# One stage of a fused transformer kernel: the ReLU's bias add goes to GpSimd, and the two copies of each expert block out of PSUM go from ScalarE to VectorE

## The chip, the cores and the metric

The kernel runs on one core of one Trainium2 chip. The metric is the device time of one execution in microseconds (us); before the change it is 1316.74 us, the median of three runs (1316.6 to 1319.15). A core has five engines that run side by side, each through its own list of instructions in order: TensorE (PE in the rows, with PEld for its weight loads), VectorE (DVE), ScalarE (ACT), GpSimd (POOL) and SyncE (SP, which only issues DMAs here). They wait for each other by semaphores. Matmul results land in PSUM; GpSimd does not touch PSUM in this kernel.

## What is computed

The reference is a two-layer network on 4 x 512 tokens of 128 features. The part that matters here is layer 0: a differential attention over 8 heads, and beside it a mixture of 8 experts, of which each token uses one:

```python
L1 = einsum(l2norm(q1), l2norm(k1)) * cos_scale;  L2 = einsum(l2norm(q2), l2norm(k2)) * cos_scale
G  = tanh(delta_gain * (L1 - L2))
A1 = softmax(L1 + G);  A2 = softmax(L2 - G)
y  = einsum(A1 - lambda_full * A2, v)             # then RMS norm, projection
...
idx = argmax(xf @ Wg.T)                           # one expert per token
h = relu(xf @ W1[e] + b1[e]);  out += (idx == e) * (h @ W2[e] + b2[e])
```

After it come a second part of layer 0 and layer 1 (a four-layer Mamba stack and a top-2 mixture of experts), which the change does not touch.

## The kernel before

The kernel is written as stages, each a `Block` in which every engine's list is written out by hand; nothing schedules the instructions but the order of the code and the semaphores. The change lies in the second stage (from about 104 to 342 us), which runs the attention of the 8 heads and, woven into it, the experts.

**Attention.** A pair of heads takes 32 steps, four steps to a unit (one batch, four key tiles), so 8 units to a pair; four pairs run one after the other. Each step needs, on TensorE, one matmul for L1 - L2 (`difference`, bank_d) and two for L1 and L2 (`scores`, bank_l); on ScalarE one tanh (`gate`, L932) and, for two steps together, one exp (`exps_of_two`, L939); on VectorE the two sums L1 + G and -L2 - G (`sums`, L988 and L989), which read bank_l. Once a unit the exps are multiplied with the values (`weigh`, L863), ScalarE copies the result out of bank_pv (`keep`, L944), TensorE transposes it (`turn`, L871) and VectorE folds it into `ybig` (`settle`, L996). `weigh` of the next unit may only write bank_pv after `settle`.

**Experts.** Tokens are sorted by expert into 24 blocks of 128 rows, one per unit of the last three pairs (the first pair instead computes the sort, writes the rows out by indirect DMA and fetches the first weights). A block goes through one PSUM bank, bank_e: TensorE transposes it (`turn_block`, L838), ScalarE copies it out (`keep_in`, L948), TensorE multiplies with W1 (`hidden`, L844), VectorE adds the bias and takes the ReLU in four instructions, one per 128 columns (`relu`, L1004), TensorE multiplies with W2 (`block_out`, L850), ScalarE copies the result out (`keep_out`, L953), SyncE stores it. GpSimd fetches the weights of the block after the next (L752, L755), once `block_out` has finished with the buffer.

**Other small work.** After each head VectorE scales its values and squares them for the RMS norm in six instructions spread over six steps (`norm_head`, L1053 to L1065). GpSimd sets up the gain and the values of the head after the next (`next_head`, L746 and L749), after the last `weigh` of the old one. SyncE loads the queries and keys of later heads, twelve DMAs per head, into XT (first head of a pair) or GATE (second).

On TensorE the order in a unit is: turn_block, weigh (first half), two differences, hidden, scores, weigh (second half), scores, two differences, block_out, scores, turn, scores. TensorE takes them strictly in that order, so a step that is not ready holds up all behind it.

Of the kernel before, what the change touches and what calls it, by code (L numbers as in the profile page):

```python
# [7 lines left out]
ALU = mybir.AluOpType  # L8
# [3 lines left out]
P = 128  # L12
# [35 lines left out]
def build_stages(nc, A, out):  # L48
    keep = ExitStack()
    with keep:  # L50
# [24 lines left out]
        with keep0:  # L75
# [556 lines left out]
            with st2:  # L632
# [44 lines left out]
                s_hn = sem("head_norm_steps")  # L677
# [9 lines left out]
                loaded = lambda q, k: q * (8 * PER) + 16 * (k // 2 + 1)  # L687

                with nc.Block() as block:
                    @block.sync  # L690
                    def _(sp):
# [48 lines left out]
                        for i in range(2):  # L740
                            sp.wait_ge(s_es[i], 16 + loaded(2, PER - 2))

                    @block.gpsimd
                    def _(pool):
# [6 lines left out]
                        def gather_weights(q, j, i, n):  # L751
# [4 lines left out]
                                                         bounds_check=NE * P - 1, oob_is_err=False).then_inc(s_wl[i], 16)  # L756

# [16 lines left out]
                        pool.sem_inc(s_cur, LEAD)  # L774
# [9 lines left out]
                        next_head(-1, 0)  # L784
                        next_head(-1, 1)

                        def turn(q, more):
# [132 lines left out]
                    def _(act):  # L920
                        for s in (s_G, s_E, s_pvs, s_xk, s_ek):
                            act.sem_inc(s, LEAD)
                        for s in s_es:
                            act.sem_inc(s, 16)
# [21 lines left out]
                        def keep_in(q, k):  # L946
                            act.wait_ge(s_xt, blk(q, k + 1))
                            nc.scalar.activation(xbT[:, :], bank_e[:, 0, :], ACT.Copy).then_inc(s_xk, 1)  # L948

                        def keep_out(q, k):  # L950
                            act.wait_ge(s_dn, blk(q, k + 1))
                            act.wait_ge(s_es[k % 2], loaded(q, k))
                            nc.scalar.activation(eo[k % 2][:, :], bank_e[:, 0, :], ACT.Copy).then_inc(s_ek, 1)  # L953

                        def pair_of_heads(q, first=False, final=False):
                            for st in range(0, STEPS, 2):
# [4 lines left out]
                                if mb == 0 and not first:  # L961
                                    keep_in(q, u)
# [3 lines left out]
                                if mb == 2 and not first:  # L966
                                    keep_out(q, u)
# [10 lines left out]
                    def _(dve):  # L978
                        for s in (s_T, s_yb, s_relu):
                            dve.sem_inc(s, LEAD)  # L980
                        link = Chain(dve, s_dch)
# [18 lines left out]
                        def relu(q, k):  # L1000
# [47 lines left out]
                        def norm_head(h, n, settled, done):  # L1048
                            seg = ybig[:, :, bass.ds(h * 34, 34)].rearrange("p t (s c) -> p t s c", s=2)
                            plus, minus = seg[:, :, 0, 0:16], seg[:, :, 1, 0:16]  # L1050
                            if n == 0:
                                dve.wait_ge(s_yb, settled)
                                nc.vector.reciprocal(rz[:, :, :].unsqueeze(3), seg[:, :, :, 16:17]).then_inc(s_hn, 1)  # L1053
                                return
                            dve.wait_ge(s_hn, done + n)
                            if n == 1:
                                nc.vector.tensor_scalar(rz[:, :, 1], rz[:, :, 1], neg_lam[:, :], None, ALU.mult).then_inc(s_hn, 1)
                            if n == 2:
                                TT(seg[:, :, :, 0:16], seg[:, :, :, 0:16], rz[:, :, :].unsqueeze(3).broadcast_to([P, NT, 2, 16]), ALU.mult).then_inc(s_hn, 1)
                            if n == 3:  # L1060
                                TT(plus, plus, minus, ALU.add).then_inc(s_hn, 1)
                            if n == 4:
                                TT(ysq[:, :, :], plus, plus, ALU.mult).then_inc(s_hn, 1)
                            if n == 5:
                                nc.vector.tensor_reduce(ms[:, :, bass.ds(h, 1)], ysq[:, :, :].unsqueeze(2), AX.X, ALU.add).then_inc(s_hn, 1)  # L1065
# [1520 lines left out]
```

## Time and profile before

| | us |
|---|---|
| median of three runs (lowest, highest) | 1316.74 (1316.6, 1319.15) |
| the profiled execution's own time | 1318.12 |
| its span, first to last instruction | 1316.3 |
| the 24 expert units, first turn_block to the last | 164.28 to 332.29 |

A row of the timeline gives the start, the duration, the engine, the source line, the operation, and in brackets how long the engine had been idle before it and what ended that wait. SPq rows are DMA issues. A row with "x8" is eight instructions merged, and its duration runs from the first one's start to the last one's end.

Over the whole span the page has TensorE busy for 87%, VectorE for 84%, ScalarE for 79% and GpSimd for 69%, at a mean granted clock of 0.953. Most of GpSimd's work lies in later stages; in this one it is idle for most of the time.

### The profile page before, as it was taken

To read this page: it belongs to the slowest core of one execution; us is meant where nothing else is said; L and a number is where in the kernel's file an instruction comes from. 1 tells how busy PE (TensorE), PEld (TensorE's weight loads), DVE (VectorE), ACT (ScalarE), POOL (GpSimd) and SP (SyncE) were. 2 spreads that over 40 slices of the span, in tenths; PEclk is the share of its full clock that TensorE was granted. 3 is DMA by queue.
4 is the path that set the end of the run, shared out by engine and by line. 5 is a ranking of instruction groups with operands and counts; after the bars stand their busy time and mean duration, and the time that the engine had idled before them with its cause. 6 is when DMAs were issued, how large, how long until landed. Compare 5 with 4: busy or idle time off the path is not lost. (4 is left out here: it accounts for less than half of the span.)

```text
span 1316.3 us, 21647 instructions
## 1 busy us (share of the span) xinstructions
PE 1145.7 (87%) x6667; PEld 611.3 (46%) x6667; DVE 1101.3 (84%) x1535; ACT 1043.2 (79%) x1804; POOL 912.4 (69%) x749
## 2 busy tenths in 40 slices
PE   6566799999719999977999999999999999999885
PEld 4461244444515656753444444444444444444442
DVE  8967899999675323339999999999999999999997
ACT  4346999999452224378999999999999999999992
POOL 6733311111473451367999999999999999999995
PEclk9786999999858999998999999999999999999998
DMA  2022233433108216434144414442442354234420
GB/s 71 33 88 95 77 107 113 126 114 104 31 23 287 88 36 163 129 85 101 54 107 106 99 45 104 104 98 56 104 112 68 74 107 113 59 77 105 107 65 16
DMA packets 89060, 120.19 MB, mean 91 GB/s; under 512 B 17869, under 2 KB 49464, under 8 KB 88576
## 3 DMA queue, kind: packets, MB, share of 16 engines
q1 hardware_dynamic: 82688, 101.59, 30.4%
q0 software_dynamic: 6272, 17.38, 4.5%
q8 instruction: 48, 0.79, 0.3%
q14 instruction: 52, 0.43, 0.1%
HBM read 92.28 MB, written 27.45 MB: 91 GB/s over the span
## 5 line engine op out<-in xcount | busy, mean ns | idle before, releaser
L2104 POOL TENSOR_TENSOR hcm<-hs,Cc 128x1024 f32<-128x1024 f32 x255 | 600.3, 2376 | 27.8 <-DVE hs L2487 19.8
L2487 DVE TENSOR_TENSOR_SCAN hs<-decay,dbx 128x512 f32<-128x512 f32 x512 | 586.9, 1201 | 25.6 <-ACT decay L2380 9.9
L2221 PEld LDWEIGHTS dbx<-ident_sb,scaled 128*128 128x128 f32 x2048 | 227.4, 142 | 288.7 <-DVE hs L2487 164.8
L2221 PE MATMUL dbx<-ident_sb,scaled 128*128 128x128 f32 x2048 | 312.1, 283 | 41.6 <-DVE hs L2487 38.2
L2362 ACT ACTIVATE scaled<-duT,BT 128x256 f32<-128x256 f32 x579 | 266.9, 506 | 0.2 <-PE dbx L2221 0.2
L2380 ACT ACTIVATE decay<-dtr_even,a_all 128x512 f32<-128x512 f32 x256 | 179.0, 723 | 3.0 <-DVE hs L2487 1.7
L2380 ACT ACTIVATE decay<-dtr_odd,a_all 128x512 f32<-128x512 f32 x256 | 177.7, 719 | 2.4 <-DMA dtr_odd<-dt_turn 1.5
L2239 PE MATMUL y_bank<-hcm,fold_sb 128*32 128x512 f32 x1024 | 138.9, 615 | 1.8 <-POOL hcm L2104 1.8
L939 ACT ACTIVATE ex<-tt 128x2048 f32<-128x2048 f32 x64 | 123.8, 1934 | 2.5 <-DVE tt L989 1.8
L2152 PE MATMUL slots<-XT,w_tap 128*128 128x512 f32 (+1 forms) x224 | 115.5, 597 | 3.1 <-DVE scaled L2478 2.9
L988 DVE TENSOR_TENSOR tt<-bank_l,gt 128x512 f32<-128x512 f32 x128 | 87.1, 681 | 12.7 <-ACT gt L932 10.9
L2089 POOL TENSOR_SCALAR scaled<-duT,BT 128x256 f32<-128x256 f32 x204 | 95.3, 479 | 0.0
L932 ACT ACTIVATE gt<-bank_d,dgh 128x512 f32<-128x512 f32 x128 | 82.7, 714 | 10.2 <-PE bank_d L817 9.2
L989 DVE SCALAR_TENSOR_TENSOR tt<-bank_l,gt 128x512 f32<-128x512 f32 x128 | 87.1, 680 | 0.0
L1849 DVE TENSOR_TENSOR hid<-sil,u_bank 128x512 f32<-128x512 f32 x32 | 22.0, 687 | 59.1 <-ACT sil L1706 37.5
L863 PE MATMUL bank_pv<-ex,v_head 128*32 128x512 f32 x512 | 69.1, 612 | 2.0 <-DVE ybig L996 1.7
L752 POOL CAST weight_rows<-w_row 128x1 uint32 (+1 forms) x24 | 4.7, 195 | 95.1 <-PE bank_e L850 95.1
L2478 DVE TENSOR_TENSOR scaled<-slots,BT 128x1024 f32<-128x1024 f32 (+1 forms) x60 | 67.9, 1131 | 0.0
L1706 ACT ACTIVATE sil<-g_bank 128x512 f32<-128x512 f32 x32 | 19.1, 597 | 47.3 <-PE u_bank L1563 47.2
L1939 DVE TENSOR_TENSOR hid<-sil,u_bank 128x320 f32<-128x320 f32 x32 | 15.6, 488 | 48.8 <-ACT sil L1792 48.8
L1527 POOL DMA_INDIRECT shares_of_tokens<-eo,to_u x18 | 17.2, 954 | 51.9 <-ACT eo L1829 48.3
L1519 POOL DMA_INDIRECT expert_rows<-XR,rows_u x32 | 31.3, 978 | 30.9 <-PE o_bank L1570 21.6
(379 smaller groups left out, 1882.3 us busy)
## 6 DMA issues: line engine op xcount, KB each, us to landing
Cc<-bc_turn SPq DMA_DIRECT2D x256, 64.0 KB, 2.2
dtr_even<-dt_turn SPq DMA_DIRECT2D x32, 512.0 KB, 8.7
dtr_odd<-dt_turn SPq DMA_DIRECT2D x32, 512.0 KB, 8.3
dt_turn<-dt SPq DMA_DIRECT2D x16, 512.0 KB, 2.8
hid<-in_conv_row SPq DMA_DIRECT2D x4, 512.0 KB, 5.4
shares_of_tokens<-zeros SPq DMA_DIRECT2D x2, 1024.0 KB, 7.9
w_rg<-in_w_rg SPq DMA_DIRECT2D x8, 256.0 KB, 3.0
w_ru<-in_w_ru SPq DMA_DIRECT2D x8, 256.0 KB, 3.8
```

What stands on the lines that cost most here:

```text
L932: nc.scalar.activation(gt[:, st % RING, :], bank_d[st % 2][:, :], ACT.Tanh, scale=dgh[:, i:i + 1]).then_inc(s_G, 1)
L939: nc.scalar.activation(ex[:, (st // 4) % 2, j:j + 2, :, :], tt[:, i:i + 2, :, :], ACT.Exp).then_inc(s_E, 2)
L988: nc.vector.tensor_tensor(tt[:, st % RING, 0, :], bank_l[st % 2][:, 0, :], gt[:, st % RING, :], ALU.add)
L989: nc.vector.scalar_tensor_tensor(tt[:, st % RING, 1, :], bank_l[st % 2][:, 1, :], -1.0, gt[:, st % RING, :], ALU.mult, ALU.subtract).then_ ...
L2089: nc.gpsimd.tensor_scalar(scaled[buffer_of(l, n, k)][:, kk, :, j, :], duT[:, n % 2, kk, :].rearrange("p (g c) -> p g c", c=32), BT[:, n % ...
L2104: nc.gpsimd.tensor_tensor(hcm[:, r - 1:r + 1, :], hs[:, p % HR - 1:p % HR + 1, :], Cc[:, k:k + 1, :].broadcast_to([P, 2, 512]), ALU.mult). ...
L2152: last = mm(dst[h][:, d:512], w_tap[:, 3 - d, P * h:P * h + P], XT[:, n % 4, 0:512 - d], start=(d == 0), stop=(d == 3))
L2221: last = nc.tensor.transpose(dbx[bank_of[p]][:, P * kk:P * kk + P], scaled[buffer_of(l, b, k)][:, kk, g, :, :].rearrange("p j c -> p (j c) ...
L2239: last = mm(y_bank[h][32 * q:32 * q + 32, :], fold[:, :], hcm[:, ring_of(l, b, p + q), :], start=False, stop=(k == 3), tile_position=(0, 3 ...
L2362: nc.scalar.activation(scaled[buffer_of(l, n, k)][:, kk, :, j, :], duT[:, n % 2, kk, :].rearrange("p (g c) -> p g c", c=32), ACT.Copy, sca ...
L2380: nc.scalar.activation(dec[:, p % DR, :], dtr[b % 2][:, g, :], ACT.Exp, scale=a_all[:, l, 4 * g + k:4 * g + k + 1]).then_inc(s_dec, 1)
L2487: nc.vector.tensor_tensor_scan(hs[:, p % HR, :], dec[:, p % DR, :], dbx[bank_of[p]][:, :], 0.0, ALU.mult, ALU.add).then_inc(s_sc, 1)
```

## The change

The change does five things, all in the second stage:

1. The bias. relu(z + b) is written as max(z, -b) + b. VectorE does the first half for all 512 columns in one instruction (`floor_at_bias`), GpSimd adds b afterwards in SBUF (`add_bias`), and only then may `block_out` start. GpSimd waits for a new semaphore, `s_floor`.
2. `keep_in` and `keep_out` move from ScalarE to VectorE. `keep_out` of the block before stands after the sums of a unit's second step and ahead of `settle`; `keep_in` stands after `settle`, ahead of the sums of the third step.
3. Four of the six instructions of `norm_head` move to GpSimd (`weigh_head`); VectorE keeps the reciprocal (steps 5 and 21) and the closing reduction (now at steps 14 and 30).
4. SyncE issues the loads of head 2 (`first_head_of_next(-1, .)`) ahead of its wait for the sorted rows, no longer behind it.
5. Semaphore counts follow. The first `keep_out` copies a bank that holds nothing yet and stores nothing; the last one stands after the pairs.

```diff
                         for part in range(2):
                             load_part(sp, 1, 1, part, s_ld[1])
+                        for part in range(2):
+                            first_head_of_next(-1, part)
                         sp.wait_ge(s_scat, 16 * NT)
                         for i in range(AHEAD):
                             load_block(i, i)
-                        for part in range(2):
-                            first_head_of_next(-1, part)
...
+                        def weigh_head(h, done):
+                            seg = head_values(h)
+                            plus, minus = seg[:, :, 0, 0:16], seg[:, :, 1, 0:16]
+                            pool.wait_ge(s_hn, done)
+                            pool.sem_inc(s_asked, 1)
+                            nc.gpsimd.tensor_scalar(rz[:, :, 1], rz[:, :, 1], neg_lam[:, :], None, ALU.mult).then_inc(s_hn, 1)
...
                         next_head(-1, 0)
+                        weigh_head(0, 1)
                         next_head(-1, 1)
+
+                        def add_bias(q, k):
+                            pool.wait_ge(s_floor, blk(q, k + 1))
+                            pool.sem_inc(s_asked, 1)
+                            nc.gpsimd.tensor_tensor(hid[:, :, :], hid[:, :, :], b1[k % 2].unsqueeze(2).broadcast_to([P, 4, P]), ALU.add).then_inc(s_relu, 1)
 
                         def turn(q, more):
                             for k in range(PER):
+                                add_bias(q, k)
+                                if k == 2:
+                                    weigh_head(q * 2 + 1, q * 12 + 7)
                                 if k == PER // 2 and more:
                                     next_head(q, 0)
+                                if k == 6:
+                                    weigh_head(q * 2 + 2, q * 12 + 13)
...
-                                if mb == 0 and not first:
-                                    keep_in(q, u)
...
-                                if mb == 2 and not first:
-                                    keep_out(q, u)
...
+                        def keep_out(q, k):
+                            dve.wait_ge(s_dn, blk(q, k + 1))
+                            dve.wait_ge(s_es[k % 2], loaded(q, k + 2))
+                            nc.vector.tensor_copy(eo[k % 2][:, :], bank_e[:, 0, :]).then_inc(s_ek, 1)
+
+                        def floor_at_bias(q, k):
                             dve.wait_ge(s_h, blk(q, k + 1))
                             dve.wait_ge(s_wl[k % 2], loaded(q, k))
-                            for f in range(4):
-                                last = nc.vector.tensor_scalar(hid[:, f, :], bank_e[:, f, :], b1[k % 2][:, f:f + 1], 0.0, ALU.add, ALU.max)
-                            last.then_inc(s_relu, 1)
+                            nc.vector.scalar_tensor_tensor(hid[:, :, :], b1[k % 2].unsqueeze(2).broadcast_to([P, 4, P]), -1.0, bank_e[:, :, :],
+                                                           ALU.mult, ALU.max).then_inc(s_floor, 1)
...
+                                if mb == 2 and not first:
+                                    keep_in(q, u)
                                 sums(q, st)
+                                if mb == 1 and not first:
+                                    keep_out(q, u - 1)
                                 if mb == 1 and not (first and u < 2):
                                     settle(q, u - 2)
...
+                                if st == 14 and not first:
+                                    mean_square(q * 2 + 1, q * 12 + 11)
```

TensorE's order is the same before and after. On VectorE a unit without norm work (the first of the last pair; bank_l0 and bank_l1 are the two banks of scores, block_out1 the buffer of the block before) stands like this before:

```order
L988 TENSOR_TENSOR tt<-bank_l1,gt 128x512
L989 SCALAR_TENSOR_TENSOR tt<-bank_l1,gt 128x512
L996 TENSOR_REDUCE ybig<-bank_pv 128x4x34
L988 TENSOR_TENSOR tt<-bank_l0,gt 128x512
L989 SCALAR_TENSOR_TENSOR tt<-bank_l0,gt 128x512
L988 TENSOR_TENSOR tt<-bank_l1,gt 128x512
L989 SCALAR_TENSOR_TENSOR tt<-bank_l1,gt 128x512
L1004 TENSOR_SCALAR hid<-bank_e,expert_weights0 128x128 x4
```

and like this after:

```order
L1006 TENSOR_TENSOR tt<-bank_l1,gt 128x512
L1007 SCALAR_TENSOR_TENSOR tt<-bank_l1,gt 128x512
L1025 COPY block_out1<-bank_e 128x128
L1014 TENSOR_REDUCE ybig<-bank_pv 128x4x34
L1020 COPY block_inT<-bank_e 128x128
L1006 TENSOR_TENSOR tt<-bank_l0,gt 128x512
L1007 SCALAR_TENSOR_TENSOR tt<-bank_l0,gt 128x512
L1006 TENSOR_TENSOR tt<-bank_l1,gt 128x512
L1007 SCALAR_TENSOR_TENSOR tt<-bank_l1,gt 128x512
L1030 SCALAR_TENSOR_TENSOR hid<-expert_weights0,bank_e 128x512
```

So one copy stands ahead of `settle`, the other between `settle` and the four sums, and one instruction of 512 columns takes the place of four of 128.

On GpSimd the first three blocks of the last pair are, before (a cast and a gather per block):

```order
L752 CAST weight_rows0<-w_row 128x1
L755 DMA expert_weights0<-in_w_expert,weight_rows0 128x1028
L752 CAST weight_rows1<-w_row 128x1
L755 DMA expert_weights1<-in_w_expert,weight_rows1 128x1028
L752 CAST weight_rows0<-w_row 128x1
L755 DMA expert_weights0<-in_w_expert,weight_rows0 128x1028
```

and after:

```order
L810 TENSOR_TENSOR hid<-hid,expert_weights0 128x512
L754 CAST weight_rows0<-w_row 128x1
L757 DMA expert_weights0<-in_w_expert,weight_rows0 128x1028
L810 TENSOR_TENSOR hid<-hid,expert_weights1 128x512
L754 CAST weight_rows1<-w_row 128x1
L757 DMA expert_weights1<-in_w_expert,weight_rows1 128x1028
L810 TENSOR_TENSOR hid<-hid,expert_weights0 128x512
L765 TENSOR_SCALAR rz2<-rz2,neg_lam 128x16
L768 TENSOR_TENSOR ybig<-ybig,rz2 128x16x2x16
L771 TENSOR_TENSOR ybig<-ybig 128x16x16
L774 TENSOR_TENSOR ysq2<-ybig 128x256
```

Each block begins with the bias add, and the norm work of a head stands behind that of the third (and seventh) block. At the turn from one pair to the next, the add of the new pair's first block stands behind `next_head`, which waits for the old pair's last `weigh`.

On SyncE, between the loads of head 1 (into GATE) and the loop, the loads of head 2 (into XT) follow the two block loads before:

```order
L109 DMA GATE<-qk_parts 8x2048
L701 DMA block_in0<-block_rows 128x128
L701 DMA block_in1<-block_rows 128x128
L107 DMA XT<-qk_parts 24x1x2048
L107 DMA XT<-qk_parts 16x1x2048
```

and precede them after:

```order
L109 DMA XT<-qk_parts 24x1x2048
L109 DMA XT<-qk_parts 16x1x2048
L109 DMA XT<-qk_parts 8x2048
L703 DMA block_in0<-block_rows 128x128
L703 DMA block_in1<-block_rows 128x128
```

The twelve loads of head 2 thus no longer stand behind the wait for the sorted rows.

## Rows read from the trace of the kernel before

**Rows 1.** Busy time by engine: 24 expert units, then one unit (window, length first)

```profile
core 0: us, PE busy (x) PEld busy (x) DVE busy (x) ACT busy (x) POOL busy (x), PEclk, DMA share, GB/s
164.28:332.29 168.01, 162.93 (x1128) 82.16 (x1128) 157.16 (x336) 158.19 (x209) 29.13 (x54) 1.00 0.37 111
310.46:317.47 7.01, 7.01 (x51) 3.58 (x50) 6.39 (x14) 6.84 (x10) 1.20 (x3) 1.00 0.32 96
```

**Rows 2.** Timeline, TensorE and VectorE in that unit (start, us, engine, line)

```profile
309.55 0.66 PE L871 MATMUL bank_pv<-ident_sb,pvs 128*128 128x128 f32 x4
...
310.25 0.44 DVE L996 TENSOR_REDUCE ybig<-bank_pv 128x136 f32<-128x272 f32 x1 [0.46 <-PE bank_pv L871]
...
310.46 0.33 PE L838 MATMUL bank_e<-ident_sb,block_in 128*128 128x128 f32 x1
...
310.84 0.69 DVE L988 TENSOR_TENSOR tt<-bank_l,gt 128x512 f32<-128x512 f32 x1 [0.16 <-ACT gt L932]
...
312.18 1.06 PE L844 MATMUL bank_e<-block_inT,expert_weights 128*128 128x128 f32 x8
...
313.28 1.13 DVE L1004 TENSOR_SCALAR hid<-bank_e,expert_weights 128x128 f32<-128x128 f32 x4
...
315.25 1.06 PE L850 MATMUL bank_e<-expert_weights,hid 128*128 128x128 f32 x8
...
317.47 0.33 PE L838 MATMUL bank_e<-ident_sb,block_in 128*128 128x128 f32 x1
```

**Rows 3.** Timeline, first and last unit with norm work; then VectorE's closing reduction, by line

```profile
171.40 0.33 PE L838 MATMUL bank_e<-ident_sb,block_in 128*128 128x128 f32 x1
...
179.38 0.33 PE L838 MATMUL bank_e<-ident_sb,block_in 128*128 128x128 f32 x1
...
325.30 0.33 PE L838 MATMUL bank_e<-ident_sb,block_in 128*128 128x128 f32 x1
...
L1065 DVE TENSOR_REDUCE ms<-ysq 128x256 f32 (+1 forms) x7 | 2.9, 410 | 0.0
```

**Rows 4.** By line: GpSimd's 128x512 instructions in stage one (busy us, mean ns)

```profile
L386 POOL TENSOR_TENSOR prod<-mh 128x512 f32<-128x512 f32 x16 | 20.0, 1278 | 4.7 <-DVE mh L229 4.7
L410 POOL TENSOR_TENSOR ACC<-XR,b_mo 128x512 f32<-128x512 f32 x4 | 4.6, 1178 | 6.6 <-DVE XR L313 6.6
```

**Rows 5.** Timeline: a handoff from VectorE to GpSimd, and the two side by side

```profile
19.73 0.56 DVE L229 TENSOR_TENSOR mh<-s_bank,b_mha 128x384 f32<-128x384 f32 x1
...
20.36 2.50 POOL L386 TENSOR_TENSOR prod<-mh 128x512 f32<-128x512 f32 x2 [1.53 <-DVE mh L229]
...
366.27 0.69 DVE L1221 TENSOR_TENSOR z<-ACC,Y 128x512 f32<-128x512 f32 x1 [1.14 <-DMA ACC<-block_outs,row_u]
...
366.47 0.55 POOL L1135 TENSOR_TENSOR off<-off,rstd 128x4 f32<-128x4 f32 x1
...
368.74 0.20 POOL L1135 TENSOR_TENSOR off<-off,rstd 128x4 f32<-128x4 f32 x1
```

**Rows 6.** Timeline, end of the first pair: loads of head 2

```profile
130.69 0.39 PE L822 MATMUL bank_l<-XT 48*128 48x512 bf16 x1 [0.22 <-DVE tt L989]
...
143.01 1.91 SPq L107 DMA_DIRECT2D XT<-qk_parts  x3
...
159.96 0.61 PE L817 MATMUL bank_d<-XT 112*128 112x512 bf16 x2 [2.27 <-DMA XT<-qk_parts]
...
160.43 1.26 ACT L932 ACTIVATE gt<-bank_d,dgh 128x512 f32<-128x512 f32 x2 [0.97 <-issue]
```

**Rows 7.** Timeline, first block of a pair: hidden, then GpSimd's next_head

```profile
166.03 1.06 PE L844 MATMUL bank_e<-block_inT,expert_weights 128*128 128x128 f32 x8
...
168.50 0.18 POOL L746 COPY dgh<-delta_gain_sb 128x1 f32<-128x1 f32 x1 [22.83 <-PE bank_pv L863]
...
168.62 0.40 POOL L749 COPY v_head<-v_tok 128x256 f32<-128x256 f32 x1
```

**Rows 8.** Timeline, the last block: relu, then block_out

```profile
335.07 1.12 DVE L1004 TENSOR_SCALAR hid<-bank_e,expert_weights 128x128 f32<-128x128 f32 x4
...
336.24 1.16 PE L850 MATMUL bank_e<-expert_weights,hid 128*128 128x128 f32 x8 [0.52 <-DVE hid L1004]
```

More of the change, by code:

```diff
@@ L756, in gather_weights @@
                                                          bounds_check=NE * P - 1, oob_is_err=False).then_inc(s_wl[i], 16)
+                        def weigh_head(h, done):
[4 more added lines that the diff above has]
+                            nc.gpsimd.tensor_scalar(rz[:, :, 1], rz[:, :, 1], neg_lam[:, :], None, ALU.mult).then_inc(s_hn, 1)
+                            pool.wait_ge(s_hn, done + 1)
+                            pool.sem_inc(s_asked, 1)
+                            nc.gpsimd.tensor_tensor(seg[:, :, :, 0:16], seg[:, :, :, 0:16], rz[:, :, :].unsqueeze(3).broadcast_to([P, NT, 2, 16]), ALU.mult).then_inc(s_hn, 1)
+                            pool.wait_ge(s_hn, done + 2)
+                            pool.sem_inc(s_asked, 1)
+                            nc.gpsimd.tensor_tensor(plus, plus, minus, ALU.add).then_inc(s_hn, 1)
+                            pool.wait_ge(s_hn, done + 3)
+                            pool.sem_inc(s_asked, 1)
+                            nc.gpsimd.tensor_tensor(ysq[:, :, :], plus, plus, ALU.mult).then_inc(s_hn, 1)
                         def next_head(q, i):
@@ L773, in _ @@
                         nc.gpsimd.memset(zeros[:, :, :], 0.0).then_inc(s_zz, 1)
-                        pool.sem_inc(s_cur, LEAD)
+                        for s in (s_cur, s_relu):
+                            pool.sem_inc(s, LEAD)
                         pool.wait_ge(s_rows, 1)
@@ L978, in _ @@
                     def _(dve):
-                        for s in (s_T, s_yb, s_relu):
+                        for s in (s_T, s_yb, s_floor, s_xk):
                             dve.sem_inc(s, LEAD)
+                        dve.sem_inc(s_ek, LEAD - 1)
+                        for s in s_es:
+                            dve.sem_inc(s, 32)
                         link = Chain(dve, s_dch)
@@ L1046, in route, with inverse_sums, mean_square @@
                                 link(nc.vector.tensor_scalar(w_row[:, :], w_row[:, :], lane[:, 0:1], None, ALU.add), s_rows)
[L1048 to L1065, printed above, removed]
+                        def inverse_sums(h, settled):
+                            dve.wait_ge(s_yb, settled)
+                            nc.vector.reciprocal(rz[:, :, :].unsqueeze(3), head_values(h)[:, :, :, 16:17]).then_inc(s_hn, 1)
+                        def mean_square(h, done):
+                            dve.wait_ge(s_hn, done)
+                            nc.vector.tensor_reduce(ms[:, :, bass.ds(h, 1)], ysq[:, :, :].unsqueeze(2), AX.X, ALU.add).then_inc(s_hn, 1)
                         def pair_of_heads(q, first=False):
@@ L1069, in pair_of_heads @@
                                 u, mb = st // 4, st % 4
+                                if mb == 2 and not first:
+                                    keep_in(q, u)
                                 sums(q, st)
+                                if mb == 1 and not first:
+                                    keep_out(q, u - 1)
                                 if mb == 1 and not (first and u < 2):
                                     settle(q, u - 2)
[L1073 to L1076 removed]
+                                if st == 5 and not first:
+                                    inverse_sums(q * 2 + 1, unit(q, 0))
+                                if st == 14 and not first:
+                                    mean_square(q * 2 + 1, q * 12 + 11)
+                                if st == 21:
+                                    inverse_sums(q * 2 + 2, unit(q, 4))
+                                if st == 30:
+                                    mean_square(q * 2 + 2, q * 12 + 17)
                                 if mb == 3 and not first:
[L1078 removed]
+                                    floor_at_bias(q, u)
                                 if first:
@@ L1085, in _ @@
                         pair_of_heads(2)
+                        keep_out(2, PER - 1)
                         settle(2, UNITS - 2)
```

26 lines of the change are left out of this document (8 added, 18 removed).

## The prediction

> **What bounds the kernel now.** I first read the busy time of the second stage, since the change touches no other. Over its 24 expert units TensorE is busy 162.93 of 168.01 us, ScalarE 158.19, VectorE 157.16, at a granted clock of 1.00; GpSimd works 29.13 us [rows 1]. Three engines are nearly full, so the next view is one unit alone: there TensorE is busy 7.01 of 7.01 us, ScalarE 6.84, VectorE 6.39 [rows 1]. In a unit without norm work TensorE's list is the bound: its steps stand back to back, 7.01 us from one turn_block to the next [rows 2]. Nothing done on another engine can make such a unit shorter; it can only make TensorE wait.
>
> The third view is where units are longer. The first unit with norm work runs from 171.40 to 179.38, 7.98 us, the last from 317.47 to 325.30, 7.83 us [rows 2, 3]. There are six, 47.8 us in all, a mean of 7.96. The other 17 of the 23 intervals share 168.01 - 47.8 = 120.2 us, a mean of 7.07. So the room is about 6 x 0.95 us of norm work plus one stall ahead of the experts: at 159.96 TensorE has waited 2.27 us for the keys and queries of head 2 [rows 6].
>
> **The change part by part.** All times below are differences within the profiled execution (span 1316.3, its own time 1318.12); I add them to the median 1316.74, since 1.4 us between the two executions does not touch a difference.
>
> *The path from turn to block_out* decides. I count from the start of turn, 309.55, as T. Before, turn_block ends at 310.79 (T+1.24), hidden starts at 312.18 (T+2.63), the ReLU runs from 313.28 to 314.41 (T+3.73 to 4.86), and block_out starts at 315.25, T+5.70 [rows 2]. It is TensorE's order that sets 5.70; the hidden values had been ready for 0.84 us. That is the slack which the change spends:
> - keep_in now stands on VectorE between settle and the sums. Settle is at T+0.70 for 0.44 us, but turn_block's result is there only at T+1.24, so keep_in starts at about T+1.29. Its price on VectorE is not in the trace; the nearest row is the ReLU itself, 128x128 out of PSUM, four in 1.13 us or 0.28 each [rows 2]; the upper end is settle's 0.44. I take 0.28. The sums start at T+1.57 (before: 310.84, T+1.29).
> - The four sums take from 310.84 to 313.28, 2.44 us [rows 2]: to T+4.01. Hidden has ended at T+3.69, so the floor starts at T+4.01.
> - The floor is one 128x512 instruction out of PSUM: 0.69 us as the sums' [rows 2], in place of 1.13. T+4.70.
> - The handoff to GpSimd: VectorE ends at 20.29 and GpSimd starts at 20.36, 0.07 us [rows 5]; for the semaphore increment that stands ahead of the add I put an estimated 0.03. T+4.80.
> - The add: 128x512 on GpSimd costs 1.18 and 1.28 us in two lines of stage one [rows 4]; 1.23. T+6.03.
> - To TensorE: 0.05, as from the last ReLU's end (336.19) to block_out (336.24) [rows 8]. T+6.08.
>
> That is 0.38 us behind T+5.70. TensorE then stands still 0.38 us in each unit, ahead of block_out, and scores, turn and the next T move with it. Nothing gives it back: the path runs from T to the next T. A quiet unit becomes 7.39 us. Bounds: with the add at 1.18, the other instructions 0.1 shorter between them and no increment the wait is about 0.15; with keep_in at 0.44, the add at 1.28 and 0.2 us lost at each of the two handoffs, about 0.85. I take 0.38, since each of its terms is the nearest row's. 17 quiet units: 17 x (7.39 - 7.07) = +5.4 us (+2.6 to +13).
>
> A page of the Trainium skill bears on the add. The trace shows the effect first: on 4 columns GpSimd takes 0.20 us at 368.74, but 0.55 at 366.47, ending at 367.02 when VectorE's 0.69 us sum of two SBUF tiles had just ended (366.96) [rows 5]. The Trainium skill (SBUF — State Buffer, "Who interferes with whom") says that VectorE with two SBUF inputs and a GpSimd instruction that reads SBUF lock each other out, and that VectorE with at most one SBUF input does not. By that rule the add is not blocked, as sums, floor and copies all read PSUM, and its price stays at 1.23.
>
> *Norm work.* The four instructions that leave VectorE took the 0.9 us. What stays is the reciprocal, mostly beside the wait for turn_block (I put 0.15), and the reduction, 0.41 [rows 3], which now lies on the path, ahead of the floor. Six long units go from 7.96 to 7.54: -2.5 us; five reductions in quiet units: +2.0. The GpSimd chain behind them (one small, one of 512 and two of 256 columns) I put at half a unit at most, over before the reduction asks. The gathers behind it are later by that, with a whole unit to spare.
>
> *Start of a pair.* The first add stands behind next_head, which waits for the old pair's last weigh. Hidden starts at 166.03 and next_head's copies end at 169.02, 2.99 us later [rows 7]; the add can start at about 3.1, where in a quiet unit it starts at T+4.80, which is 2.17 behind hidden. Three pairs x 0.93 = +2.8 us.
>
> *The last block* has no cover: block_out at 336.24 follows the ReLU of 335.07 at once [rows 8]. The floor is later by keep_in's 0.28 and the reduction's 0.41, and then 0.69 + 0.10 + 1.23 + 0.05 follow: 337.83, +1.6 us.
>
> *Loads of head 2.* They go out at 143.01; the last score matmuls on XT are at 130.69 [rows 6], so they can go out 12 us earlier and the stall of 2.27 us ends. ScalarE, which is next there, was idle for 0.97 us [rows 6]: gain between 0.97 and 2.27, I take 1.6. The block loads that now follow wait for the sorted rows anyway.
>
> *ScalarE's two copies* gain nothing: it is not the bound of a quiet unit. keep_out on VectorE falls into the 0.46 us in which VectorE waits for settle [rows 2]; without that cover it would cost 0.28 a unit.
>
> Sum: +5.4 - 2.5 + 2.0 + 2.8 + 1.6 - 1.6 = +7.7 us, 1324.4 us.
>
> **The rivals.**
> *Faster: the add hides.* If the path from T to block_out comes out 0.38 us shorter, because the sums close up once ScalarE's gates come earlier (VectorE waited 0.16 us for one [rows 2]) and floor and copy cost less than their neighbours, then TensorE's 7.01 holds: 17 x (-0.06) = -1.0, six long units -5.7, starts 3 x 1.3 = +3.9, the last block +1.2, loads -1.6, and the reductions vanish in slack: -3.2, 1313.5 us. It decides at a path of 5.70 us. For it: the pieces overlap a little in the rows. Against: three more instructions in one chain.
> *Much slower: the add is held up on GpSimd.* If VectorE keeps it out for one of its 0.69 us instructions, as in the row above, it costs 24 x 0.69 = 16.6 us more: 1341. Against it speaks that no VectorE instruction beside it reads two SBUF tiles.
> *No change:* a wait of about 0.1 us instead of 0.38 takes 0.28 x 23 = 6.4 us off: +1.3, 1318.0.
>
> **How the numbers follow.** Chances: the forecast, with its wait of 0.2 to 0.85 us, 0.64; held up 0.08; no change 0.14; faster 0.14. A measurement of this kernel tells 0.2%, some 2.6 us, from no change. So faster 0.14, within 0.14, slower 0.72. For 8 in 10 I leave out about 0.12 below and 0.08 above: 1314 covers the no-change case and the edge of the faster one, 1334 the forecast's upper bounds for the quiet units and two thirds of the rest.
>
> **What would show it.** In the changed trace block_out should wait for GpSimd's add in nearly every unit, some 0.4 us, and turn_block follow turn_block at about 7.4 us in quiet units; at three starts of a pair the wait should be about 1.3. GpSimd's add should read 1.2 us; 1.9 speaks for the lock. The wait for XT at 160 should be gone, and no unit reach 7.9 by norm work. If TensorE waits nowhere at block_out, my path is too long and the kernel is faster. I would also be wrong if the reductions had to wait for GpSimd's chain.

## The result, and the profile after

The changed kernel takes 1327.71 us (median of four runs, 1327.08 to 1328.89) against 1317.38 (four runs, 1316.6 to 1319.15): a ratio of 1.007, 95% interval 1.0054 to 1.0085. It is slower by some 9 us by the ratio, 10 by the medians; the forecast was 1324.4.

The busy time by engine of the changed kernel, columns as in [rows 1]: the 24 units, then a quiet unit, then one with the closing reduction of the norm.

```profile
core 0: us, PE busy (x) PEld busy (x) DVE busy (x) ACT busy (x) POOL busy (x), PEclk, DMA share, GB/s
164.73:337.84 173.11, 167.08 (x1128) 80.69 (x1128) 150.09 (x288) 150.44 (x163) 67.99 (x100) 1.00 0.35 107
301.24:308.47 7.23, 7.23 (x51) 3.49 (x50) 6.39 (x13) 6.41 (x8) 4.02 (x5) 1.00 0.36 109
308.47:316.03 7.56, 7.27 (x51) 3.50 (x49) 6.72 (x14) 6.83 (x8) 3.09 (x7) 1.00 0.30 87
```

VectorE has lost 7 us of work and ScalarE 8, and the 24 units are 5.1 us longer than in [rows 1]. So the load fell and the time rose: a wait was made. The waits over the last three pairs name it (what waited, what ended the wait, us in all, times, longest):

```profile
POOL hid L810 <- DVE hid L1030: 51.7, 21, 3.3
PEld bank_e L880 <- POOL hid L810: 17.0, 24, 2.7
PE bank_e L880 <- POOL hid L810: 5.8, 9, 1.8
```

block_out (L880) waits for GpSimd's add (L810) in each of the 24 blocks, with its weight load if not with the matmul itself. The timeline of the quiet unit answers [rows 2]; turn starts at 300.33:

```profile
300.33 0.66 PE L901 MATMUL bank_pv<-ident_sb,pvs 128*128 128x128 f32 x4
...
301.24 0.33 PE L868 MATMUL bank_e<-ident_sb,block_in 128*128 128x128 f32 x1
...
301.60 0.29 DVE L1020 COPY block_inT<-bank_e 128x128 f32<-128x128 f32 x1
301.81 0.68 DVE L1006 TENSOR_TENSOR tt<-bank_l,gt 128x512 f32<-128x512 f32 x1
...
304.20 0.68 DVE L1030 SCALAR_TENSOR_TENSOR hid<-expert_weights,bank_e 128x512 f32<-128x512 f32 x1
...
305.06 1.03 POOL L810 TENSOR_TENSOR hid<-hid,expert_weights 128x512 f32<-128x512 f32 x1 [2.84 <-DVE hid L1030]
...
306.15 0.97 PEld L880 LDWEIGHTS bank_e<-expert_weights,hid 128*128 128x128 f32 x8 [0.46 <-POOL hid L810]
306.15 1.16 PE L880 MATMUL bank_e<-expert_weights,hid 128*128 128x128 f32 x8
...
308.47 0.33 PE L868 MATMUL bank_e<-ident_sb,block_in 128*128 128x128 f32 x1
```

And from the trace of the kernel before, the weight loads of block_out in the unit of [rows 2], whose matmuls start at 315.25:

```profile
315.04 1.08 PEld L850 LDWEIGHTS bank_e<-expert_weights,hid 128*128 128x128 f32 x8
```

From T = 300.33 the copy starts at T+1.27, the sums at T+1.48, the floor at T+3.87, the add at T+4.73, block_out at T+5.82. TensorE's own order would have allowed T+5.70. The wait is only 0.12 us, but there is a second loss: before, the first weight load of block_out ran ahead under the matmuls before it (315.04, matmuls from 315.25), and now it starts only when hid is complete, together with the first matmul (306.15); block_out takes 1.16 us instead of 1.06. Together 0.22, and the unit is 7.23 us long instead of 7.01.

This unit lies in the last pair. The two pairs with experts before it run in a loop (below: the loops), and there TensorE's own order is longer: 7.12 to 7.14 us a quiet unit and block_out at T+5.82 or 5.83, in the kernel with norm work and loads alone (below). The changed kernel has T+5.83 and 7.23 to 7.25 us there. So in the quiet units of the loops nothing to speak of is left of the wait, and the added 0.1 us is the weight load.

The same view at the third start of a pair, to be read beside [rows 7]:

```profile
287.43 1.06 PE L874 MATMUL bank_e<-block_inT,expert_weights 128*128 128x128 f32 x8
...
290.01 0.18 POOL L748 COPY dgh<-delta_gain_sb 128x1 f32 x1 [3.22 <-PE bank_pv L893]
290.14 0.39 POOL L751 COPY v_head<-v_tok 128x256 f32 x1
290.50 1.03 POOL L810 TENSOR_TENSOR hid<-hid,expert_weights 128x512 f32<-128x512 f32 x1
291.59 0.97 PEld L880 LDWEIGHTS bank_e<-expert_weights,hid 128*128 128x128 f32 x8 [1.42 <-POOL hid L810]
291.59 1.16 PE L880 MATMUL bank_e<-expert_weights,hid 128*128 128x128 f32 x8 [0.93 <-POOL hid L810]
```

Here the add stands in GpSimd's list behind next_head, which waits for weigh (L893). And the last block, beside [rows 8]:

```profile
341.13 0.67 DVE L1030 SCALAR_TENSOR_TENSOR hid<-expert_weights,bank_e 128x512 f32<-128x512 f32 x1
341.98 1.04 POOL L810 TENSOR_TENSOR hid<-hid,expert_weights 128x512 f32<-128x512 f32 x1 [3.34 <-DVE hid L1030]
...
343.08 1.16 PE L880 MATMUL bank_e<-expert_weights,hid 128*128 128x128 f32 x8 [1.81 <-POOL hid L810]
```

By line (count, busy us, mean ns), the new instructions:

```profile
L810 POOL TENSOR_TENSOR hid<-hid,expert_weights 128x512 f32<-128x512 f32 x24 | 24.8, 1035 | 51.9 <-DVE hid L1030 51.7 <-issue 0.2
L1030 DVE SCALAR_TENSOR_TENSOR hid<-expert_weights,bank_e 128x512 f32<-128x512 f32 x24 | 16.2, 676 | 0.2 <-PE bank_e L874 0.2
L1025 DVE COPY block_out<-bank_e 128x128 f32<-128x128 f32 x25 | 7.3, 291 | 8.3 <-PE bank_e L880 7.2
L1020 DVE COPY block_inT<-bank_e 128x128 f32<-128x128 f32 x24 | 6.6, 275 | 1.3 <-PE bank_e L868 0.3
```

**Where the time went.** I count the stage from the start of the first sums to the start of the last settle. Before, in two traces, it is 237.2 and 238.4 us; after, 242.9 and 242.8. That is +5.0 of the 9 to 10. The 23 intervals from turn_block to turn_block, sorted by kind, in the first trace of each:

| intervals | before | after | difference | predicted |
|---|---|---|---|---|
| six with norm work before | 47.76 | 44.89 | -2.9 | -2.5 |
| five with the reduction now | 35.57 | 37.85 | +2.3 | +3.6 |
| three starts of a pair | 21.50 | 25.25 | +3.75 | +3.75 |
| nine others | 63.18 | 65.12 | +1.9 | +2.9 |
| sum | 168.01 | 173.11 | +5.1 | +7.7 |

(The prediction's 0.32 for each of 17 quiet units is shared out over the last three kinds.) The other 4 us or so lie behind the stage, in code that the change does not touch; the last experiment looks there.

### The profile page after: what moved, and what is told of

Same layout as the page of the kernel before. It is cut to its first block and busy times, and to the rows that moved or that the text cites. A ratio compares the mean times of both kernels' runs of the same rounds, so it can differ in the third digit from the quotient of the medians.

```text
span 1326.1 us, 21646 instructions
## 1 busy us (share of the span) xinstructions
PE 1155.3 (87%) x6667; PEld 614.8 (46%) x6667; DVE 1093.4 (82%) x1484; ACT 1034.6 (78%) x1756; POOL 955.7 (72%) x801
## 5 line engine op out<-in xcount | busy, mean ns | idle before, releaser
L893 PE MATMUL bank_pv<-ex,v_head 128*32 128x512 f32 x512 | 69.5, 616 | 2.7 <-DVE ybig L1014 2.0
L810 POOL TENSOR_TENSOR hid<-hid,expert_weights 128x512 f32<-128x512 f32 x24 | 24.8, 1035 | 51.9 <-DVE hid L1030 51.7
L1730 ACT ACTIVATE sil<-g_bank 128x512 f32<-128x512 f32 x32 | 19.1, 597 | 47.4 <-PE u_bank L1587 47.3
```

## The experiments

Two theories stood against each other at first: the add lies on the path that ends a unit (mine), or the two copies on VectorE do the harm. Ratios are to the kernel before, timed on the same chip (1318.79 and 1318.85 us in the two timed comparisons). The changed kernel was timed in another comparison, in which the kernel before had 1317.38; so a difference to its 1327.71 is uncertain by some 1.4 us, and the stage in the traces is the finer measure.

### The ReLU back on VectorE

The changed kernel, but the bias and ReLU again in four VectorE instructions; copies, norm work and loads stay as changed.

```diff
-                                add_bias(q, k)
...
-                                    floor_at_bias(q, u)
+                                    relu(q, u)
```

> The changed kernel with the bias and ReLU back on VectorE in four instructions; the two copies stay on VectorE, the norm work on GpSimd and the early loads stay. Chain theory (GpSimd's add at the end of the chain turn, copy, sums, floor, add is what TensorE waits for): the hidden values are ready at about T+5.0, ahead of T+5.70, so TensorE no longer waits at block_out; quiet units go from 7.23 to 7.0 us, starts of pairs from 8.1 to 8.9 back to 7.1 to 7.4, the 23 unit intervals from 173.1 to about 162 us, the time to 1311 to 1316 us. Rival (the two copies in VectorE's list delay the sums and so TensorE): quiet units stay above 7.2 us and the time above 1322 us.

Measured: 1315.22 us, ratio 0.9967 (0.9952 to 0.9982). It takes 12.5 us off the changed kernel, 9.7 of them in the stage (233.2), and is faster than the kernel before with both copies on VectorE. Units of the last pair are 6.98 to 7.01 us, 7.17 with the reduction. The copies do hardly any harm alone: the kernel with norm work and loads alone, further down, differs from this one only in having them on ScalarE, and its stage is 0.6 us shorter (232.6, one trace each). What costs is floor and add.

### The copies back on ScalarE

```diff
-                                if mb == 2 and not first:
-                                    keep_in(q, u)
...
-                                if mb == 1 and not first:
-                                    keep_out(q, u - 1)
```

> The changed kernel with the two copies back on ScalarE at their old places; GpSimd's bias add, the norm work on GpSimd and the early loads stay. Chain theory: the sums start 0.2 us earlier, floor at about T+3.7, add done at T+5.65, right at the edge of T+5.70: quiet units 7.0 to 7.1 us, starts of pairs still long (8.0 to 8.9), the 23 intervals about 167 us, the time about 1321 us. Rival (the copies are the whole cost): the time falls below 1314 us. Second rival (the add alone is the cost, wherever the copies are): it stays at 1326 us or more.

Measured: 1321.68 us, ratio 1.0024 (1.0013 to 1.0034); 239.8 us in the stage, 3.1 less. Quiet units of the last pair are 7.09 to 7.14. In the loops the units stayed at 7.24 to 7.40, longer than I expected. The gain there came from the units with a reciprocal (7.39 for 7.56) and with the reduction (7.25 for 7.57); the quiet ones are 7.31, even 0.08 longer than in the changed kernel. In them hidden ends at T+3.82 (last pair T+3.69), VectorE waits 0.25 us for it, and the floor starts at T+3.94 where it started at T+3.87. So the copy ahead of the sums costs something, but only where the sums, and not hidden, hold up the floor, and where the add already ends the path: in the run above it cost next to nothing.

### next_head behind the first add

```diff
                                 add_bias(q, k)
+                                if k == 0:
+                                    next_head(q - 1, 1)
...
-                            if more:
-                                next_head(q, 1)
```

> The changed kernel with GpSimd's set-up of the second head of the next pair behind the bias add of that pair's first block, no longer ahead of it. If the three long units at the starts of pairs (8.11, 8.94, 8.20 us) come from the add waiting behind that set-up, they fall by about 0.9 each and the time by 2.7 to 1325 us, with the other units as they are. If they come from the loop's turn or from instruction supply, nothing changes (1327.7).

Measured: 1324.49 us, ratio 1.005 (1.0033 to 1.0067), 3.2 off the changed kernel. The three starts are 7.26, 7.43 and 7.24 us instead of 8.11, 8.94 and 8.20. The fifth units of the two loop pairs are longer (7.57 and 7.34 for 7.25 and 7.24), all others unchanged. The timeline of the second start shows the add at 1.97 us behind hidden, and next_head behind it:

```profile
225.43 1.06 PE L873 MATMUL bank_e<-block_inT,expert_weights 128*128 128x128 f32 x8
...
227.40 1.03 POOL L809 TENSOR_TENSOR hid<-hid,expert_weights 128x512 f32<-128x512 f32 x1 [2.94 <-DVE hid L1029]
228.38 0.18 POOL L748 COPY dgh<-delta_gain_sb 128x1 f32 x1
...
228.50 1.15 PE L879 MATMUL bank_e<-expert_weights,hid 128*128 128x128 f32 x8
```

### Both of these mends

> The changed kernel with two parts undone together: the copies back on ScalarE, and GpSimd's next_head of a pair's end moved behind the add of the new pair's first block. Alone the one gave -6.0 us against the changed kernel and the other -3.2. My theory, they are separate places and add up: -9, about 1318.5, ratio 1.000; the starts of a pair near 7.2. Rival, they share slack (with the copies gone the starts have less to lose): -7, 1321, ratio 1.002.

Measured: 1320.15 us, ratio 1.0006 (0.9994 to 1.0018). In the stage 237.1 us, 5.8 less than changed, where the two alone gave 3.1 and 3.0: they nearly add up there. The time is 7.6 us below the changed kernel's, between my 9 and the rival's 7, so it does not decide. The 9 us of the expectation came from adding medians, and the medians also carry what differs behind the stage.

### The add twice

```diff
+                            nc.gpsimd.tensor_tensor(spare[:, :, :], hid[:, :, :], b1[k % 2].unsqueeze(2).broadcast_to([P, 4, P]), ALU.add)
                             nc.gpsimd.tensor_tensor(hid[:, :, :], hid[:, :, :], b1[k % 2].unsqueeze(2).broadcast_to([P, 4, P]), ALU.add).then_inc(s_relu, 1)
```

> The changed kernel with a second bias add of the same size on GpSimd (its result goes to a spare tile and is used by nothing) ahead of the real one. My theory, the add lies on the path that ends each unit: block_out starts one add (1.03 us) later in every unit, so quiet units go from 7.23 to 8.26 us, units with a reduction from 7.56 to 8.59, and the 24 blocks together give +24.7 us against the changed kernel, about 1352. Rival, the added wait is set by something else (semaphores, TensorE's weight loads, the copies) and the add has slack: less than +5 us, units at 7.3 to 7.4.

Measured: 1349.68 us (one run). The 24 units, columns as above:

```profile
163.23:359.26 196.03, 168.20 (x1127) 80.70 (x1127) 150.07 (x288) 153.42 (x164) 90.94 (x123) 1.00 0.30 95
```

That is 22.9 us more over 23 intervals, 1.00 each: 8.23 for 7.23, 8.56 for 7.56. One unit of the timeline:

```profile
313.27 1.03 POOL L811 TENSOR_TENSOR spare<-hid,expert_weights 128x512 f32<-128x512 f32 x1 [2.93 <-DVE hid L1032]
314.26 1.04 POOL L812 TENSOR_TENSOR hid<-hid,expert_weights 128x512 f32<-128x512 f32 x1
...
315.36 1.16 PE L882 MATMUL bank_e<-expert_weights,hid 128*128 128x128 f32 x8 [1.06 <-POOL hid L812]
```

The two adds start 0.99 us apart, and all of it reaches the end of the unit. The add has no slack.

### Half the add

```diff
-nc.gpsimd.tensor_tensor(hid[:, :, :], hid[:, :, :], b1[k % 2].unsqueeze(2).broadcast_to([P, 4, P]), ALU.add)
+nc.gpsimd.tensor_tensor(hid[:, 0:2, :], hid[:, 0:2, :], b1[k % 2][:, 0:2].unsqueeze(2).broadcast_to([P, 2, P]), ALU.add)
```

> The changed kernel with the bias added to two of the four groups of 128 hidden columns only; the other two stay floored at -b, so the output is not the reference's. My theory: the add falls from 1.03 to some 0.55 us, the path from turn to block_out from T+5.82 to T+5.34, below TensorE's own 5.70, so the quiet units fall to TensorE's 7.01 (7.12 in the loops) and no further; the reduction's units lose 0.33 to 0.45, the three starts and the last block 0.5 each: about -8 us, 1319 to 1320. Rival, the path has no such floor (TensorE is held by the add whatever it costs): 0.48 a unit, -11.5 us, 1316. Rival, the cost lies in the handoffs and not in the add: no unit shorter than 7.2, 1326.

Measured: 1320.98 us (one run), 235.5 us in the stage, 7.4 less than changed. The add by line:

```profile
L810 POOL TENSOR_TENSOR hid<-hid,expert_weights 128x256 f32<-128x256 f32 x24 | 14.6, 608 | 53.6 <-DVE hid L1030 53.4 <-issue 0.2
```

It is 0.43 us shorter, but the quiet units of the last pair gain only 0.22: they are at 7.01 us, TensorE's own, and those of the loops at 7.13, TensorE's own there. The path has the floor that the prediction put at T+5.70. A unit with the reduction loses the whole 0.43 (7.13 for 7.56 in the last pair), as expected, which brings it almost down to that floor.

### The whole add, in two halves

All of the bias, but in two instructions of 256 columns with a semaphore each; block_out's first two groups of matmuls wait for the first only.

```diff
+                            pe.wait_ge(s_half, blk(q, k + 1))
                             for f in range(4):
+                                if f == 2:
+                                    pe.wait_ge(s_relu, blk(q, k + 1))
```

> The changed kernel with the whole bias add kept on GpSimd, but in two instructions of 256 columns, and block_out's first two groups of matmuls wait for the first one only. Half an add took 0.61 us. My theory: block_out can start 0.42 us earlier, so TensorE's own order is the bound again (7.01 us a unit in the last pair, 7.13 and 7.31 in the loops), as where half the bias was left out: in the stage 235.5 to 236, -7 us against the changed kernel, about 1320, ratio 1.000 to 1.002. Rival, the second half comes too late and TensorE waits in the middle of block_out: the units stay at 7.2 or more, 1325 to 1327.

Measured: 1320.15 us, ratio 1.0007 (0.9998 to 1.0017), 236.8 us in the stage. The timeline of a quiet unit:

```profile
312.71 0.68 DVE L1034 SCALAR_TENSOR_TENSOR hid<-expert_weights,bank_e 128x512 f32<-128x512 f32 x1
...
313.58 1.18 POOL L812 TENSOR_TENSOR hid<-hid,expert_weights 128x256 f32<-128x256 f32 x2 [2.85 <-DVE hid L1034]
...
314.54 1.06 PE L884 MATMUL bank_e<-expert_weights,hid 128*128 128x128 f32 x8
```

block_out starts before the second half is done (314.76), waits for nothing and takes 1.06 us again. The two halves take 1.18 us together, more than the one add of 1.03, and yet the units of the last pair are 7.00 to 7.04 us (7.26 with the reduction). The weight loads run ahead again (from 314.32). The stage is 0.8 us longer than expected; the units with the reduction are 7.26 where half the add had 7.13.

### All three mends

> All three mends of the changed kernel at once: the add in two halves, the copies back on ScalarE, next_head behind the first add. My theory: no unit and no start is longer than TensorE's own order makes it, in the stage about 233, as the kernel that has norm work on GpSimd and the early loads but the ReLU on VectorE (232.6): 1314 to 1315, ratio 0.997. That would show that the add on GpSimd can be hidden, and that it then gains nothing over the ReLU on VectorE. If taking the ReLU off VectorE were worth something by itself, it would come out below 1312.

Measured: 1315.28 us, ratio 0.9969 (0.9958 to 0.998), 233.2 us in the stage. With the next experiment it tells what the add on GpSimd is worth.

### Norm work and loads alone

The kernel before, with only the four norm instructions on GpSimd and the early loads of head 2.

> The kernel before with two parts of the change alone: four norm instructions per head on GpSimd, and the early loads of head 2; bias, ReLU and copies as before. If the six long units of before came from the norm instructions in VectorE's list, every unit takes 7.0 to 7.1 us, the 23 intervals about 162 instead of 168 us, and with 1 us from the loads the time is about 1310 us. If part of the added time of the changed kernel lies outside this stage and belongs to any shift of the program (4 us), it is about 1314 us.

Measured: 1313.52 us, ratio 0.9958 (0.9941 to 0.9974), the fastest of all, 5 us under the kernel before. Its 24 units and those of the three mends:

```profile
163.06:327.19 164.13, 162.19 (x1128) 82.72 (x1128) 149.68 (x311) 157.27 (x208) 45.47 (x78) 1.00 0.36 113
```

```profile
163.73:327.77 164.04, 162.01 (x1128) 82.56 (x1128) 140.19 (x242) 157.42 (x208) 71.14 (x123) 1.00 0.36 113
```

With the ReLU on VectorE 149.68 us of VectorE's work, with the add on GpSimd 140.19, and the same time: 164.13 and 164.04. TensorE is busy for 162 of them. Taking the ReLU off VectorE buys nothing, even where it costs nothing.

The time is 3.5 us above the 1310 of my expectation mostly because the units of the loops did not come down to 7.1 (the former six long ones are 7.30 to 7.34 there, 7.01 in the last pair). It is not a shift behind the stage, which the expectation allowed for: that stretch has 975.7 us, 1 us more than before. So two of the change's five parts alone are worth 5 us, and the other three turn this gain into a loss.

### Early loads alone

> The kernel before with one part of the change alone: SyncE issues the loads of head 2 ahead of its wait for the sorted rows. In the changed kernel TensorE's wait of 2.27 us for them is gone and the stretch from the first sums to the first turn_block is 0.7 us shorter. My theory: about -0.9 us, ratio 0.9993, not to be told from no change by the time; in the trace the wait at about 160 us is gone. My prediction's figure was -1.6.

Measured: 1318.62 us, ratio 0.9996 (0.9987 to 1.0006): not to be told from no change. The trace shows the effect: at the first matmul on head 2's keys, where [rows 6] have 2.27 us of waiting, there is none for a DMA:

```profile
157.06 0.61 PE L817 MATMUL bank_d<-XT 112*128 112x512 bf16 x2
```

From the first sums to the first turn_block it is 58.8 us here, 59.1 and 59.0 in the two traces of the changed kernel, 59.8 and 60.9 in the two of the kernel before. (All twelve traces with the early loads have 58.6 to 59.1.) So -0.7 to -1.9 for the change, of which the shorter end is nearer to what the time shows.

### The two kernels again

> The kernel before once more, unchanged, for a second trace. In the first pair of traces the changed kernel lost 5.7 us inside the second stage and about 4 us elsewhere, in code that the change does not touch. If those 4 us are run to run, this trace's time outside the stage (first sums to span end less the stage) lies somewhere in 974.6 to 977.6 us. If they belong to the changed kernel, it is at 974.6 to 975 again.

> The changed kernel once more, unchanged, for a second trace. Inside the stage 242.9 us again, give or take 0.3. Outside the stage: if the extra 3 to 4 us were run to run, 974.6 to 976.5 us and a time near 1325; if they belong to the changed kernel, 977 to 978 again and a time of 1327 to 1329.

Measured: 1321.15 and 1329.8 us (one run each). Inside the stage the changed kernel repeats to 0.1 us. Behind it, from the last settle to the span's end, the kernel before has 974.6 and 974.9 us, the changed one 977.5 and 979.8. The kernels with part of the change have 974.8 to 976.2, the add twice 976.9, half the add 979.5. So both traces of the changed kernel have the extra, and its times ask for it too, since the stage gives only 5 of their 9 to 10 us; but two traces of each kernel are few, and its size wanders by 2 us (ahead of the stage both wander, from 104.5 to 106.0 us). One part of it can be placed. In layer 1's experts TensorE waits for gathered rows (xg). Six microseconds behind that wait, first before, then after (TensorE's busy time, granted clock, DMA share, GB/s), and the two microseconds of the latter with the lowest clock:

```profile
520.30:526.30 6.00, 6.00 (x31) 1.00 0.68 194
```

```profile
527.80:533.80 6.00, 6.00 (x20) 0.72 0.33 89
530.00:532.00 2.00, 2.00 (x5) 0.50 0.20 43
```

The waits themselves, in the two timelines, and a pair of matmuls behind each:

```profile
520.30 0.64 PE L1653 MATMUL x_bank<-ident_sb,xg 128*128 128x128 f32 x3 [0.88 <-DMA xg<-expert_rows]
...
521.51 0.70 PE L1662 MATMUL u_bank<-xgT,w_ru 128*128 128x320 f32 x2
```

```profile
527.76 0.64 PE L1677 MATMUL x_bank<-ident_sb,xg 128*128 128x128 f32 x3 [1.63 <-DMA xg<-expert_rows]
...
530.77 1.27 PE L1686 MATMUL u_bank<-xgT,w_ru 128*128 128x320 f32 x2
```

Why the rows land later with the changed kernel is open: the kernels with part of the change have 0.98 to 1.40, the add twice 1.51. Some 1.3 us more lie behind the start of the last scan (19.1 and 19.5 us against 18.3 and 17.9), but the kernels of the experiments have 18.4 to 20.1 there, in no order that follows the parts of the change; its cause is open.

## Why the prediction was right, and where it was wrong

The direction was right, and so was the path: the add twice and half the add show that floor, handoff and add set block_out, and that TensorE's order is the floor under them. The size of the wait was wrong, and that the time came out near the forecast is luck in part. By steps:

- **The path.** Predicted T+6.08, measured T+5.82. The add was mis-sized: 1.23 by [rows 4], where it took 1.03. The copy costs 0.21 in VectorE's list (301.60 to 301.81), not 0.28, and the sums 2.39 instead of 2.44. The handoff was too cheap: 0.18 us from the floor's end (304.88) to the add, not 0.10; the 0.03 in it for the increment came from no row.
- **The wait.** Predicted 0.38 a unit; it is 0.12 in the last pair (at most 0.01 in the loops), and 0.10 for the weight load that no longer runs ahead, which the prediction did not have. A quiet unit is 7.23 us, not 7.39. These two errors partly cancel; the nine quiet units gave +1.9 instead of +2.9. The lower bound was added up wrongly too: by its own terms 0.38 less 0.05, 0.10 and 0.03 is 0.20, not 0.15. The measured wait lies below either; taken alone it is the "about 0.1 us" of the no-change rival. What kept the stage above that rival's +1.3 is mostly the weight load, which neither had.
- **Norm work.** Six long units -2.9 (predicted -2.5). The reduction costs 0.33 a unit (7.56 against 7.23), not 0.41; together with the shorter path the five units gave +2.3 instead of +3.6. That it lies on the path was right, and no reduction waited for GpSimd's norm work.
- **Starts of a pair.** +3.75, as predicted, though the three are uneven (+0.99, +1.57, +1.19). The add starts 2.95, 3.31 and 3.07 us behind hidden, predicted 3.1. Moving next_head behind the add gave 3.0 of them back in the stage, which shows the cause.
- **The last block.** From turn_block to block_out 5.24 us, before 3.95: +1.3 (predicted +1.6).
- **Loads of head 2.** Predicted -1.6; between -0.7 and -1.9, alone too little for the time to show.
- **ScalarE's copies.** keep_out on VectorE is hidden, as predicted: with the ReLU back, units without a reduction are no longer than TensorE's order.
- **The lock on GpSimd.** It did not come: 24 adds have a mean of 1035 ns (1029 to 1044) while VectorE's sums run beside them, which read one operand from PSUM. The rule of the Trainium skill (SBUF — State Buffer, "Who interferes with whom"), by which a VectorE instruction with at most one SBUF input, outside its 2-port modes, does not contend with GpSimd, agrees with that. Its other half, two SBUF inputs, was not tried beside an add.

So in the stage the sum was +7.7 and the traces show +5.0 (+5.7 in the first pair of traces). Of the 2.6 us by which the intervals fell short, 1.0 lies in the nine quiet units, 1.3 in the five with the reduction and 0.4 in the six with norm work before. That the time still came out 3 us above the forecast, not below, is due to the 4 us behind the stage, of which the prediction had none: it held that the change touches no other stage. The median lies in the range, but the two errors have opposite signs, and only one of them was in the working: the path carried the direction, luck the closeness of the figure.

## What to carry to other kernels

Work moved off a full engine helps only where that engine ends the wait: here VectorE lost 7 us of work and the unit followed TensorE and a chain of handoffs. When one step on a path is split between two engines, price the whole path (each handoff, and the weight load that used to run ahead), and let the consumer start on the first half: two halves cost 0.15 us more on GpSimd and freed 0.22 us a quiet unit of the last pair on TensorE, 0.10 in the loops. Try the parts of a change apart: norm work and loads alone gained 5 us, which the rest hid. Before a queue takes over a step of the path, look at what already waits in it: a copy that was harmless (next_head) cost a microsecond or so at each start of a pair.

## What the runs showed of the hardware

- GpSimd's 128x512 add with a broadcast operand, in place, took 1035 ns, 128x256 took 608; the nearest instructions of stage one took 1278 and 1178 [rows 4].
- Eight fp32 matmuls took 1.06 us where their first weight load started 0.21 us ahead of them, and 1.15 to 1.16 us in all 24 blocks of the changed kernel, where it had to wait for its operand and started with them.
- At one place, between stretches in which TensorE was busy, waits of 1.63, 1.79 and 1.95 us were followed by the lower clock, and eleven of 0.88 to 1.51 were not. There 0.75 us more of waiting (1.63 against 0.88) came with about 2.2 us more in all.
- In the two loops units take 7.12 and 7.30 us where those of the last pair take 7.01, with the same instructions (norm work and loads alone). The difference lies between turn_block and the first half of weigh, which starts 0.39 us behind it in the loops (191.65 to 192.04), 0.28 in the last pair (306.16 to 306.44), and 0.59 in the units of 7.30 (198.77 to 199.36, of which the trace puts 0.25 down to settle); what holds it up in the others is open.
